# Transformer block in fp32 on one core: the order of TensorE's feed-forward work redrawn, with its banks, its gates and the router's power

## The reference

```
logits = xt @ Wr + br                       # xt: normalised tokens, 8 experts
top_p, top_idx = top_k(softmax(logits), 2)  # weights = top_p / sum(top_p)
xn = layernorm(xt)
h = gelu(einsum('end,edh->enh', xn*ln_g + ln_b, W1) + b1)      # hidden 256
y = einsum('enh,ehd->end', h, W2) + b2
out = t + (weights * y of the two chosen experts).sum()
```

## Time and profile before

| | |
|---|---|
| time, median of 3 runs | 56.42 us (56.4 to 56.81) |
| time of the profiled execution | 56.28 us |
| its span, first to last instruction | 54.5 us |
| TensorE matmuls busy | 49.7 us (91%) |
| VectorE busy | 37.5 us (69%) |
| ScalarE busy | 32.0 us (59%) |
| GpSimd busy | 18.8 us (35%) |
| 14 of the 16 first layers (L960) | 224 matmul records |
| the six second layers (L996) | 384 records |
| the four tails (L1014) | 128 records |

### The profile page before, as it was taken

How to read it: one execution, slowest core, us unless ns; L and a number is a source line. 1 busy time by engine, 2 the same in 40 slices (tenths; PEclk the granted TensorE clock), 3 DMA queues, 4 the chain that set the end, 5 groups by cost and what they waited for, 6 DMA issues and landing times.

```text
span 54.5 us, 2448 instructions
## 1 busy us (share of the span) xinstructions
PE 49.7 (91%) x976; PEld 36.8 (67%) x976; DVE 37.5 (69%) x171; ACT 32.0 (59%) x75; POOL 18.8 (35%) x44
## 2 busy tenths in 40 slices
PE   4999979999968899999999999999999999999900
PEld 2332646976746795597577799896758997599800
DVE  3098689699999795999626899839910319748920
ACT  4600386993796959994499990100699701994000
POOL 4129588000055499996529990000000000000000
DMA  0351366967000000000000000000011000000022
GB/s 0 96 127 19 78 144 137 375 222 268 12 6 0 6 0 0 12 0 0 0 0 18 0 0 12 0 0 12 0 48 48 12 0 0 12 0 6 12 48 48
DMA packets 2940, 2.42 MB, mean 44 GB/s; under 512 B 2032, under 2 KB 2544, under 8 KB 2928
## 3 DMA queue, kind: packets, MB, share of 16 engines
q1 hardware_dynamic: 2608, 2.23, 13.5%
q10 hardware_dynamic: 320, 0.03, 0.5%
HBM read 2.00 MB, written 0.26 MB: 41 GB/s over the span
## 4 chain that ended last, share of the span: by engine, by line
PE 83%; DVE 8%; issue 2%; ACT 1%; DVEq 0%; ACTq 0%
PE banks L960 24%; PE banks L996 22%; PE banks L820 9%; PE banks L1014 7%; PE banks L858 4%; PE banks L937 3%; PE banks L837 3%; PE banks L887 2%; PE banks L902 2%; PE banks L866 2%; PE banks L828 2%; PE banks L845 2%; DVE nmax L529 1%; PE banks L977 1%; DVE res L706 1%
## 5 line engine op out<-in xcount | busy, mean ns | idle before, releaser
L431 ACT ACTIVATE H<-banks,PF 128x512 f32<-128x512 f32 x32 | 19.3, 708 | 7.8 <-PE banks L960 7.3
L960 PE MATMUL banks<-XE,W1F 64*64 64x256 f32 x224 | 13.7, 382 | 0.0
L996 PEld LDWEIGHTS banks<-W2F,H 128*64 128x64 f32 x384 | 11.6, 138 | 1.3 <-issue 1.2
L996 PE MATMUL banks<-W2F,H 128*64 128x64 f32 x384 | 12.2, 223 | 0.0
L960 PEld LDWEIGHTS banks<-XE,W1F 64*64 64x64 f32 x224 | 7.9, 133 | 3.4 <-issue 0.6
L321 POOL TENSOR_SCALAR XE<-XF,PF,LB 128x256 f32<-128x256 f32 x14 | 7.8, 567 | 1.6 <-ACT XF L409 1.6
L820 PE MATMUL banks<-const-bfloat16-1.0 128*128 128x512 bf16 x11 | 4.9, 615 | 0.8 <-PEq L1124 0.8
L299 POOL TENSOR_TENSOR rs<-base,half 128x2 f32<-128x2 f32 x4 | 2.8, 701 | 6.9 <-DVE base L570 6.8
L392 ACT ACTIVATE PR<-banks,nmax 128x256 f32<-128x256 f32 x8 | 3.8, 481 | 1.3 <-DVE nmax L529 1.2
L658 DVE TENSOR_TENSOR prod<-banks,gate 128x512 f32<-128x512 f32 x4 | 2.8, 690 | 2.3 <-PE banks L996 2.3
L1014 PEld LDWEIGHTS banks<-W2F,H 128*64 128x64 f32 x128 | 3.9, 138 | 0.5 <-issue 0.4
(11 more groups left out here) (81 smaller groups left out, 69.4 us busy)
## 6 DMA issues: line engine op xcount, KB each, us to landing
W1F<-in_w_dram SPq DMA_DIRECT2D x1, 768.0 KB, 4.5
W2F<-in_w_dram SPq DMA_DIRECT2D x1, 512.0 KB, 4.7
W1F<-in_w_dram SPq DMA_DIRECT2D x1, 256.0 KB, 3.4
X<-in_x_dram SPq DMA_DIRECT2D x2, 64.0 KB, 1.9
X<-in_x_dram SPq DMA_DIRECT2D x1, 128.0 KB, 2.3
B2D<-in_b_dram SPq DMA_DIRECT2D x8, 2.0 KB
out_dram<-res SPq DMA_DIRECT2D x1, 128.0 KB, 1.7
out_dram<-res SPq DMA_DIRECT2D x2, 64.0 KB, 1.8
```

Source lines behind the costliest of these rows:

```text
L431: nc.scalar.activation(H[:, r, :].rearrange("p (t n) -> p t n", t=PT), ps_z[z_slot(g // J)][:, :, PIX * j:PIX * j + PIX], ACT.Gelu, bias=P ...
L960: mm = nc.tensor.matmul(ps_z[z_slot(q)][C * c:C * c + C, k, PIX * j:PIX * j + PIX], W1F[rows, e, j, C * c:C * c + C], XE[h][rows, e, :], s ...
L996: mm = nc.tensor.matmul(ps_y[s % 2][C * c:C * c + C, k, n, :], H[:, (2 * J * s + J * k + j) % RING, left:left + C], W2F[:, J * (2 * p + k) ...
```

## The change

Nothing of the arithmetic changes but the way in which the gates are turned and multiplied by b2. In TensorE's list:

- `layer1(3)` goes ahead of `attend(3)`. First layers 4 to 7 stand in one row, and `turn_x2(3)` behind them.
- `layer2(1)` and `layer2(2)` follow, then `logits(1)` and first layers 8 to 10. `layer2(3)` and `layer2(4)` are one pair, and `turn_gates` comes behind them.
- `bias` stands between first layers 11 and 12, and 13 to 15 follow it without a second layer between them. `layer2(5)` goes behind first layer 15, directly ahead of the four tails.
- `turn_gates` is two plain matmuls of the gates by the identity, one for each half of the array's columns, so that the turned gates are in rows 0 to 63 and again in 64 to 127; `bias` is four matmuls of 64 x 64 where it was two of 32 x 128. B2D has 128 rows, and its eight small loads go to other rows.

The banks and the waits follow: slots and predecessors of first layers 9 to 15, the logits of half 1 in banks 2 and 3, `turn_x2(3)` in bank 4, other banks for the tails. On VectorE `sum_tokens(3)` moves behind `route(0, 7)`; `weigh(1)` and `add_up(1)` go ahead of the rest of half 1's routing; the two `add_bias` go behind `weigh(4)`. On ScalarE the copies, `tanh(1)` and the gates' copy move to later GELUs. On GpSimd `router_pow(0)` goes ahead of the first stretches.

```diff
-    return {1: 0, 2: 0, 9: 7, 10: 8}.get(q, q - 3)
+    return {9: 7, 13: 11, 14: 12, 15: 10}.get(q, q - 3)
...
-    return (0, 1, 2, 3, 1, 2, 3, 1, 2, 1, 2, 3, 1, 2, 3, 1)[q]
+    return (0, 1, 2, 3, 1, 2, 3, 1, 2, 1, 3, 2, 1, 2, 1, 3)[q]
...
-        ps_x2 = [banks[:, k, 0:P] for k in (2, 2, 5, 5)]
-        ps_L = [... for k in (2, 4)]
-        ps_gates = banks[0:HALVES * TILES * E, 2, 0:P]
+        ps_x2 = [banks[:, k, 0:P] for k in (2, 2, 5, 4)]
+        ps_L = [... for k in (2, 2)]
+        ps_gates = banks[:, 2, 0:P]
...
-                   for used in ((4, 4, 5, 5), (6, 6, 7, 7), (4, 4, 5, 5), (6, 7, 0, 1))]
+                   for used in ((4, 4, 6, 6), (7, 7, 5, 5), (4, 4, 6, 6), (7, 5, 0, 2))]
...  GpSimd
             second_pow(1)
+            router_pow(0)
             stretch_second(0)
             stretch_second(1)
             stretch(0, 2)
-            router_pow(0)
             stretch(0, 3)
...  ScalarE
             turn_x2(2)
-            for g in range(8, 10):
+            for g in range(8, 12):
                 gelu(g)
             turn_x2(3)
-            for g in range(10, 14):
+            for g in range(12, 18):
                 gelu(g)
             tanh(1)
-            for g in range(14, 18):
+            for g in range(18, 22):
                 gelu(g)
             turn_gates()
-            for g in range(18, HALVES * UNITS):
+            for g in range(22, HALVES * UNITS):
...  VectorE
             weigh(0)
+            weigh(1)
+            add_up(1)
             for stage in range(2, 11):
                 route(1, stage)
-            weigh(1)
-            add_up(1)
             weigh(2)
             add_up(2)
             weigh(3)
+            add_up(3)
+            add_halves(0)
+            weigh(4)
             add_bias(0)
             add_bias(1)
-            add_up(3)
-            add_halves(0)
             finish_first()
-            weigh(4)
             weigh(5)
...  TensorE
             def turn_gates():
                 pe.wait_ge(gate_ready, HALVES)
-                pe.wait_ge(h_ready, J * 7)
-                nc.tensor.transpose(ps_gates, gate[...], ident[:, :]).then_inc(gates_ps, 1)
+                pe.wait_ge(h_ready, J * 11)
+                for c in range(2):
+                    nc.tensor.matmul(ps_gates[C * c:C * c + C, :], gate[...], ident[:, :],
+                                     start=True, stop=True).then_inc(gates_ps, 1)
...
                 for h in range(HALVES):
-                    rows = slice(TILES * E * h, TILES * E * h + TILES * E)
-                    nc.tensor.matmul(ps_bias[h]..., gateT[rows, :], B2D[rows, :, :]..., ...)
+                    rows = slice(C * h, C * h + C)
+                    for c in range(2):
+                        nc.tensor.matmul(ps_bias[h][C * c:C * c + C, :, :]..., gateT[rows, C * c:C * c + C],
+                                         B2D[rows, :, :]..., ...)
...  layer2
                 if s == 1:
-                    pe.wait_ge(scaled_ready, HALVES)
+                    pe.wait_ge(XF_ready, IMAGES - 1)
+                if s == 2:
+                    pe.wait_ge(XF_ready, IMAGES)
...  layer2_tail
                 if k == 0:
+                    pe.wait_ge(prod_ready, STEPS - 3)
+                    pe.wait_ge(h_ready, J * 14)
+                if k == 1:
                     pe.wait_ge(prod_ready, STEPS - 2)
...  the list
             layer1(2)
+            layer1(3)
             attend(3)
-            layer1(3)
             layer2(0)
             turn_x2(2)
             layer1(4)
             layer1(5)
+            layer1(6)
+            layer1(7)
             turn_x2(3)
-            layer1(6)
-            logits(1)
-            layer1(7)
-            layer1(8)
             layer2(1)
             layer2(2)
-            turn_gates()
-            layer2(3)
-            bias()
+            logits(1)
+            layer1(8)
             layer1(9)
             layer1(10)
+            layer2(3)
+            layer2(4)
+            turn_gates()
             layer1(11)
+            bias()
             layer1(12)
-            layer2(4)
-            layer2(5)
             layer1(13)
             layer1(14)
             layer1(15)
+            layer2(5)
             for k in range(4):
                 layer2_tail(k)
```

More of the change, by code:

```diff
@@ L93, in build_block @@
         ps_O = [banks[:, k, 0:P].rearrange("p (t c) -> p t c", t=PT) for k in (3, 2, 3, 5)]
-        ps_x2 = [banks[:, k, 0:P] for k in (2, 2, 5, 5)]
-        ps_L = [banks[:, k:k + PT, 0:IMG * E].rearrange("p t (i e) -> p i t e", i=IMG) for k in (2, 4)]
-        ps_gates = banks[0:HALVES * TILES * E, 2, 0:P]
+        ps_x2 = [banks[:, k, 0:P] for k in (2, 2, 5, 4)]
+        ps_L = [banks[:, k:k + PT, 0:IMG * E].rearrange("p t (i e) -> p i t e", i=IMG) for k in (2, 2)]
+        ps_gates = banks[:, 2, 0:P]
         ps_bias = [banks[:, 2 + h, 0:PIX].rearrange("p (n c) -> p n c", c=C) for h in range(HALVES)]
@@ L111, in build_block @@
         LB = sb("LB", [P, E])
-        B2D = sb("B2D", [HALVES * TILES * E, TILES, C])
+        B2D = sb("B2D", [P, TILES, C])
         W1F = sb("W1F", [P, E, J, P])
@@ L159, in build_block @@
         gate = sb("gate", [P, HALVES, TILES, E])
-        gateT = sb("gateT", [HALVES * TILES * E, P])
+        gateT = sb("gateT", [P, P])
         H = sb("H", [P, RING, TOK])
@@ L277, in _ @@
                 for n in range(TILES):
-                    top_row = E * (TILES * h + n)
+                    top_row = C * h + E * (TILES * h + n)
                     sp.dma_start(B2D[top_row:top_row + E, n, :], b2[0, :, :]).then_inc(b2_in, 16)
@@ L419, in turn_gates @@
             def turn_gates():
-                act.wait_ge(gates_ps, 1)
+                act.wait_ge(gates_ps, 2)
                 nc.scalar.copy(gateT[:, :], ps_gates).then_inc(gateT_ready, 1)
@@ L670, in add_bias @@
             def add_bias(h):
-                dve.wait_ge(bias_ps, HALVES)
+                dve.wait_ge(bias_ps, 2 * HALVES)
                 dve.wait_ge(t_ready, IMAGES)
@@ L779, in _ @@
             route(0, 4)
-            sum_tokens(3)
             route(0, 5)
             second_norm(2)
+            route(0, 6)
+            route(0, 7)
+            sum_tokens(3)
             second_stats(3)
-            route(0, 6)
             second_moments(3)
-            route(0, 7)
             second_variance(3)
@@ L899, in turn_x2 @@
                     pe.wait_ge(XF_ready, i)
-                if i >= IMG:
+                if i == 2:
                     pe.wait_ge(t_ready, IMAGES)
+                if i == 3:
+                    pe.wait_ge(prod_ready, 1)
                 nc.tensor.transpose(ps_x2[i], X2[i // IMG][:, n:n + PT, :].rearrange("p t c -> p (t c)"),
@@ L910, in logits @@
                 else:
-                    pe.wait_ge(prod_ready, 1)
+                    pe.wait_ge(h_ready, J * 7)
                 for i in range(IMG):
@@ L915, in logits @@
                             rows = slice(C * t, C * t + C)
-                            mm = nc.tensor.matmul(banks[C * k:C * k + C, 2 + 2 * h + t, E * i:E * i + E],
+                            mm = nc.tensor.matmul(banks[C * k:C * k + C, 2 + t, E * i:E * i + E],
                                                   XF[h][rows, i, C * k:C * k + C], WR[rows, t, :],
@@ L953, in layer1 @@
                     pe.wait_ge(h_ready, J * (z_before(q) + 1))
-                if q == 11:
+                if q == 10:
+                    pe.wait_ge(scaled_ready, HALVES)
+                if q == 15:
                     pe.wait_ge(base_ready, HALVES)
@@ L967, in turn_gates @@
                 pe.wait_ge(gate_ready, HALVES)
-                pe.wait_ge(h_ready, J * 7)
-                nc.tensor.transpose(ps_gates, gate[:, :, :, :].rearrange("p h t e -> p (h t e)"), ident[:, :])\
-                    .then_inc(gates_ps, 1)
+                pe.wait_ge(h_ready, J * 11)
+                for c in range(2):
+                    nc.tensor.matmul(ps_gates[C * c:C * c + C, :], gate[:, :, :, :].rearrange("p h t e -> p (h t e)"),
+                                     ident[:, :], start=True, stop=True).then_inc(gates_ps, 1)
             def bias():
@@ L975, in bias @@
                 for h in range(HALVES):
-                    rows = slice(TILES * E * h, TILES * E * h + TILES * E)
-                    nc.tensor.matmul(ps_bias[h].rearrange("p n c -> p (n c)"), gateT[rows, :],
-                                     B2D[rows, :, :].rearrange("p n c -> p (n c)"), start=True, stop=True,
-                                     tile_position=(TILES * E * h, 0)).then_inc(bias_ps, 1)
+                    rows = slice(C * h, C * h + C)
+                    for c in range(2):
+                        nc.tensor.matmul(ps_bias[h][C * c:C * c + C, :, :].rearrange("p n c -> p (n c)"),
+                                         gateT[rows, C * c:C * c + C], B2D[rows, :, :].rearrange("p n c -> p (n c)"),
+                                         start=True, stop=True).then_inc(bias_ps, 1)
```

## The result

The changed kernel takes 58.11 us (median of 4 runs, 57.92 to 58.35) against 56.41 us for the kernel before beside it (4 runs, 56.12 to 56.81). The ratio is 1.0299, with a 95% interval of 1.0224 to 1.0374: slower. The forecast was 57.8 us, 57.0 to 58.7. The profiled execution took 57.92 us, with a span of 56.1 us against 54.5. Times and ratios leave out one execution in the chip's slower state, of 56.72 us in experiment 1.

What follows compares the result with a forecast made beforehand. TensorE's list was taken as the path. Tails at 47.77 plus 5.6 us put the last write at 53.37 against 51.86, 1.51 later; added to the profiled 56.28 this gave 57.8 us, range 57.0 to 58.7.

Steps and rivals of the forecast that it cites:

- TensorE's list: TensorE's new order walked from 20.36 us: tails start at 47.02 if nothing waits, 0.63 earlier than in the kernel before.
- The waits of layers 13 and 14: First layers 13 and 14 wait for GELUs in shared slots, losing 0.25 and 0.46 us; tails then start at 47.77.
- `bias`: Four 64 x 64 matmuls on TensorE, half of a first layer: 0.46 us, bounds 0.31 and 0.92.
- `turn_gates`: Two plain matmuls turning the gates on TensorE: kept at 0.23 us, bounds 0.12 and 0.92.
- change of shape: On TensorE, a row of any length costs about 0.1 us for going over to another shape.
- The first rival: No wait at slots 1 and 2: tails start at 47.02, time 57.1 us; chance 0.08.
- The estimate from it: Rival: gates' plain matmuls cost four times the transpose, 0.92 us, 0.7 later, 58.5 us in all; chance 0.06.
- What I took as free: `router_pow(0)` moved ahead, half 1's later routing and `layer2(4)`'s wait: each 0, bounds 0.1 and 0.3 us.
- The tail: VectorE's chain behind `layer2(5)`, uncovered: last `res` write 5.6 us behind the tails' start, against 4.21 before.
- The pause: TensorE stands 1.4 us ahead of tail 2, whose banks wait for tail 0's four `weigh_tail`.
- the rival of a clock that falls there: Clock falls to 1.2 GHz after TensorE's pause: tails 2 and 3 up to 2 us more; chance 0.06, shared with late routing.

Runs made afterwards that it cites:

- experiment 1: Changed kernel with `layer2(5)` moved between first layers 12 and 13, all else kept: 55.76 us, ratio 0.9858 against the kernel before.
- experiment 6: Kernel before with its transpose of the gates written as one plain matmul by the identity: 56.02 us in one run.
- experiment 2: Kernel before with only `layer2(5)` moved from behind `layer2(4)` to behind first layer 15: 58.39 us, ratio 1.0314 against the kernel before.
- experiment 3: Changed kernel with tails 2 and 3 in other banks, so tail 2 does not wait for VectorE: 57.72 us, ratio 1.0205 against the kernel before.
- experiment 5: Changed kernel with `layer2(5)` moved between first layers 14 and 15: 57.23 us, ratio 1.0173 against the kernel before.

## Why the prediction was right

**TensorE's list.** Walked to 47.02 for the tails without waits, and 47.77 with them; measured 47.65. The waits of layers 13 and 14 lie behind layers 12 and 13: each of these takes 1.30 us to the start of the next in place of 0.92, which makes 0.38 and 0.38, 0.76 in all, where I had 0.25 and 0.46. Layer 13 starts 2.65 us behind layer 11 and layer 14 2.60 behind layer 12, where I had 2.55 for both. ScalarE's GELUs from layer 11 on run without a gap:

```profile
41.14 6.33 ACT L431 ACTIVATE H<-banks,PF 128x512 f32<-128x512 f32 x10 [0.83 <-PE banks L964]
```

That is 1.27 us a layer. Without the two waits the tails would have started at 46.89. The difference to 47.02 lies mostly in the start, 0.05 earlier, and in `attend(3)`, whose distance to `layer2(0)` is 0.52 and not 0.61, because no change of shape follows. `bias` took 0.43 (forecast 0.46). `turn_gates` took 0.32 (forecast 0.23), within its bounds; it now stands ahead of a change of shape, which I had not charged to it. The 0.1 that I gave to a row of any length for its change of shape shows only in short rows: a first layer alone took 1.03 and 1.10, but rows of three and four took 2.75 and 3.68, which is 0.92 a layer with nothing left. The sum does not suffer, since it used the rows' whole distances. (The first rival's 57.1 us should be 57.0 by its own terms.) The Trainium skill, "TensorE: Matmul & The Clock Gate", section Terms, says of transpose mode that it is four times faster for fp32. The estimate from it was 0.92 us for the plain form; the trace does not agree for this shape, with 0.32 for both matmuls, nor does experiment 6.

**What I took as free was free.** `router_pow(0)` ran from 17.01 to 18.02 and the stretch behind it started at 18.15 (18.20 before). `layer2(4)` did not wait: half 1's gates were made from 33.38 to 36.28, 2.90 us and not 3.79, and `weigh(2)` had ended at 37.07, ahead of the need at about 37.74. The rows fit the reason that I gave, GpSimd being done by then (34.25), though no run moved the stretches alone. These are the same two stages (`hot` at L624 and `part` at L639) of half 1 in the kernel before, under stretches, and in the changed one, behind them:

```profile
31.10 0.55 DVE L624 TENSOR_TENSOR hot<-iota,topf 128x32 f32<-128x32 f32 x2
...
32.14 0.62 DVE L639 TENSOR_TENSOR part<-hot,wab 128x32 f32<-128x32 f32 x2
```

```profile
35.26 0.29 DVE L624 TENSOR_TENSOR hot<-iota,topf 128x32 f32<-128x32 f32 x2
...
35.95 0.30 DVE L639 TENSOR_TENSOR part<-hot,wab 128x32 f32<-128x32 f32 x2
```

In the changed kernel `add_up(1)` runs beside the stretches and took 0.93 us in place of 0.69, and the eight stretches took 4.74 in place of 4.38, neither on the path. The Trainium skill, "SBUF — State Buffer", section "Who interferes with whom", says that a VectorE `tensor_tensor` with both inputs in SBUF contends with GpSimd's reads. The trace agrees for the instructions shown (0.55 for two in place of 0.29) and for `add_up(1)`, but not for each: `LG` at L602, which also adds two SBUF tensors, took 0.19 us beside the stretches in both kernels (at 29.22 and 33.60), as it did for half 0.

**The tail.** The mechanism was as put, and experiments 1, 2, 3 and 5 show it; the term was sized 0.3 us too small. I had 5.6 us from the tails' start to the last `res` write against 4.21, 1.39 more. Measured by the first `res` write it is 5.32 against 3.63, 1.69 more. The missing 0.3: `weigh(5)` starts 0.24 behind the tails' start, not 0.14. It starts 2.16 us behind the start of `layer2(5)` in experiments 1 and 5 and here alike; the tail, being of the same shape, merely starts 0.1 sooner than a first layer would. From `weigh(5)` to the first `weigh_tail` is 2.44 us and not 2.37. The first four `weigh_tail`, each behind the one before, took 0.98 us (50.33 to 51.31 in the chain) and not 0.84. The three errors add to 0.31. The pause came out at 1.56 us in place of 1.4.

```profile
50.73 0.27 DVE rest L706
51.00 0.02 issue
51.01 0.29 DVE rest L706
51.31 0.04 issue
51.35 1.62 PE banks L1025 x48
52.98 0.10 DVE res L706
```

That is the changed kernel's chain (start us, us, what) over the pause: it passes through VectorE's `rest` into tail 2 and out to `res`. The granted clock stayed at 1.00 through the pause, which rules out the rival of a clock that falls there (columns as in the earlier trace rows, the clock behind the five engines):

```profile
47.65:51.35 3.70, 2.14 (x70) 1.98 (x66) 3.24 (x9) 0.00 (x0) 0.00 (x0) 1.00 0.00 0
51.35:53.60 2.25, 2.08 (x64) 1.95 (x64) 2.20 (x12) 0.00 (x0) 0.00 (x0) 1.00 0.04 11
```

**The sum**: 0.05 for the list from its first whole first layer on and 1.69 for the tail, less 0.05 for the earlier start, is 1.69 us. The profiled times differ by 1.64 (57.92 - 56.28), and the medians by 1.70. That 57.8 comes so close to the profiled 57.92 is in part luck: the tails' start was forecast 0.12 us too late and the tail 0.30 too short. The median, 58.11, lies 0.3 above the forecast, of which 0.13 is the kernel before's own profiled execution under its median (56.28 against 56.41). The rest of the change is worth keeping: with `layer2(5)` back under the first layers it is 1.4% faster than the kernel before. How that gain divides among bias, gates and fewer changes of shape was not tried part by part.

## What to carry to other kernels

An engine that has filled its list without a gap can still be given a worse order: before a piece is moved to the end, add up what the other engines do with its result before they can touch the next one, and ask what runs over that. Here 2.4 us of VectorE's work had three first layers over it, and one move took them away. A gap on the engine that bounds need not be the thing to remove: taking out the 1.56 us pause alone gave back 0.22. And where two pairs of banks are used in turn, a round of the producer must last as long as the reader holds a pair, or it waits; here two first layers make 1.84 us and the pair came free 2.6 us after the start of the layer that filled it.

## What was not expected of the hardware

A plain fp32 matmul by the identity with 64 columns of weights had its two records 0.11 us apart, with the first record of the following matmuls between them, where the transpose of the same data took 0.23 us to the next piece (experiment 6, one run). VectorE's 128 x 64 weighings of PSUM start 0.19 us apart in the four `res` writes (four in 0.85 us, each 0.27 long), and the first four behind `add_base` took 0.98 us; what held these is not shown.
